# Slot attention's first and last round: the order of five engines' work around them

## What is computed

```python
x = x + 0.5 * L0_ffn(ln(x))     # mixture of 8 experts, top 2          phase moe_a
x = x + L0_attn(ln(x))          # causal linear attention, 16 heads    phase linatt
x = x + 0.5 * L0_ffn(ln(x))     #                                      phase moe_b
x = x + 0.5 * L1_ffn(ln(x))     # gated FFN, both operands fp4-rounded phase ffn_a
x = x + L1_attn(ln(x))          # softmax attention over the 8 batches phase att
x = x + 0.5 * L1_ffn(ln(x))     #                                      phase ffn_b

# L1_attn takes S = 8 (the batches) as its sequence: each token position ("slot")
# has 16 heads whose 8 x 8 scores run over the batches
scores = einsum('sbd,tbd->bst', q, k) * scale;  attn = softmax(scores)
ctx = einsum('bst,tbd->sbd', attn, v);  out = ctx @ out_proj.T + bias
# L1_ffn: h = silu(q4(x) @ q4(w_gate).T) * (q4(x) @ q4(w_up).T);  out = q4(h) @ q4(w_down).T
# q4 rounds blocks of 16 values to an fp4 grid times the block's scale
```

## Time and profile before

| what | us |
|---|---|
| median of 3 runs (lowest, highest) | 759.08 (758.55, 763.17) |
| the profiled execution | 757.82 |
| its span in the profile | 756.0 |
| busy in the span: PE, DVE, ACT, POOL | 673.3, 606.9, 458.5, 294.7 |
| mean granted TensorE clock | 0.959 of 2.4 GHz |

### The profile page before, as it was taken

How to read it: one execution, slowest core, us unless ns; L and a number is a source line. 1 busy time by engine, 2 the same in 40 slices (tenths; PEclk the granted TensorE clock), 3 DMA queues, 4 the chain that set the end, 5 groups by cost and what they waited for, 6 DMA issues and landing times.

```text
span 756.0 us, 16397 instructions
## 1 busy us (share of the span) xinstructions
PE 673.3 (89%) x5826; PEld 481.9 (64%) x5826; DVE 606.9 (80%) x1554; ACT 458.5 (61%) x867; POOL 294.7 (39%) x417
## 2 busy tenths in 40 slices
PE   4999999789999879999997789898978987799996
PEld 2777776567888757777764456565646556456664
DVE  2788787846766678887786999999999997899983
ACT  3787788674674328777786476757454433666642
POOL 5000120156556310011013677554534527668520
PEclk9999999879999989999999799999999998899996
DMA  8000000000000000000000000000000000000000
GB/s 207 22 0 0 0 1 1 0 3 4 2 0 3 4 1 1 0 0 0 0 1 2 0 1 0 1 2 0 3 0 0 0 0 1 0 29 15 24 19 29
DMA packets 13461, 7.08 MB, mean 9 GB/s; under 512 B 1177, under 2 KB 13409, under 8 KB 13409
## 3 DMA queue, kind: packets, MB, share of 16 engines
q1 hardware_dynamic: 11328, 5.33, 2.6%
q10 hardware_dynamic: 2080, 1.05, 0.5%
HBM read 4.28 MB, written 2.10 MB: 8 GB/s over the span
## 4 chain that ended last, share of the span: by engine, by line
PE 61%; DVE 18%; ACT 10%; issue 7%; POOL 3%; DMA 1%; DVEq 0%; POOLq 0%; ACTq 0%
PE ps L1427 56%; DVE shared L1267 4%; DVE shared L1239 3%; PE ps L1778 2%; DVE x_sb L1070 2%; ACT ffn_work L533 2%; ACT ffn_work L723 2%; PE ps L1435 1%; DVE stats L985 1%; ACT xnT L584 1%; ACT x_sb L832 1%; PE ps L1441 1%; ACT ffn_work L571 1%; ACT hqT L828 1%; DVE ps L1259 1%
## 5 line engine op out<-in xcount | busy, mean ns | idle before, releaser
L1427 PEld LDWEIGHTS ps<-w_sb,sq_h 128*128 128x128 f32 x1024 | 132.3, 193 | 70.6 <-ACT sq_h L599 51.8
L1070 DVE SCALAR_TENSOR_TENSOR x_sb<-ps,gates,x_sb 128x128 f32 (+1 forms) x512 | 147.2, 344 | 24.2 <-PE ps L1427 20.3
L1427 PE MATMUL ps<-w_sb,sq_h 128*128 128x128 f32 x1024 | 138.5, 279 | 1.8 <-ACT sq_h L599 1.8
L1427 PE MATMUL ps<-xnT,w_sb 128*128 128x512 f32 x256 | 135.7, 614 | 0.0
L353 POOL TENSOR_SCALAR vareps<-meanvar 128x4 f32<-128x4 f32 (+1 forms) x28 | 8.9, 319 | 265.7 <-DVE meanvar L994 265.3
L595 ACT ACTIVATE relu_h<-ps 128x512 f32<-128x512 f32 x128 | 75.6, 591 | 56.5 <-PE ps L1427 56.2
L599 ACT ACTIVATE sq_h<-relu_h 128x512 f32<-128x512 f32 x128 | 80.6, 630 | 4.0
L1427 PE MATMUL ps<-gateT,xnT 128*128 128x352 f32 x128 | 58.9, 544 | 14.7 <-ACT ffn_work L723 13.0
L577 ACT ACTIVATE xn<-x_sb,shift,rstd 128x128 f32 (+1 forms) x136 | 57.0, 481 | 10.1 <-POOL shift L361 8.3
L400 POOL TENSOR_TENSOR shared<-shared 128x128 f32<-128x128 f32 x112 | 51.0, 455 | 27.7 <-ACT shared L678 19.5
L1427 PE MATMUL ps<-downT,hqT 128*128 128x128 f32 x384 | 57.5, 289 | 4.2 <-ACT hqT L828 3.9
(11 more groups left out here) (166 smaller groups left out, 1355.9 us busy)
## 6 DMA issues: line engine op xcount, KB each, us to landing
x_sb<-in_L_attn_x_dram SPq DMA_DIRECT2D x8, 256.0 KB, 7.5
out_dram<-x_sb SPq DMA_DIRECT2D x8, 256.0 KB, 2.3
w_sb<-in_L_ffn_w_all_dram ACTq DMA_DIRECT2D x2, 512.0 KB, 6.5
wraw<-in_L_attn_qkv_w_dram SPq DMA_DIRECT2D x1, 192.0 KB, 4.4
wraw<-attn_in_proj_weight_dram SPq DMA_DIRECT2D x1, 192.0 KB, 3.3
fraw<-in_L_ffn_w_down_dram SPq DMA_DIRECT2D x1, 176.0 KB, 3.1
fraw<-in_L_ffn_w_gate_dram SPq DMA_DIRECT2D x1, 128.0 KB, 2.7
fraw<-in_L_ffn_w_up_dram SPq DMA_DIRECT2D x1, 128.0 KB, 2.4
```

The costliest lines, as they stand in the source:

```text
L1070: t = nc.vector.scalar_tensor_tensor(tile_b(i, j), bank(4 + e % 4, TPB, C)[:, j, :], gates[:, j, e:e + 1], tile_b(i, j), ALU.mult, ALU.add)
L1427: return nc.tensor.matmul(o, a, b, start=start, stop=stop, **kw)
```

## The change

It moves instructions; it adds and takes away none but waits. PE and ACT: score(0, 0) and its copy stand in the last body of ffn_a, score and copy of half 0 of every other round at the end of the round before. In the last round x_transposes and gate_up of tile 0 (with bank 3 for the gate) stand behind context 1, the other three gate_up ahead of contexts 4 to 7. ACT's evac_xnT goes ahead of normal(1), silu of tile 0 ahead of ctx_half(0), and ctx_half(1) behind the other silu, x_squares(1) and x_offsets(1). POOL's x_back(0) goes from behind pair 3 to behind pair 1, DVE's x_snap(0) from behind pv 3 to behind pv 1. In moe_b, the statistics in group 6 go from behind accumulate(5) to behind accumulate(4).

```diff
@@ POOL, the last round of att
                     slot_pairs(s, TPB - 1, 0, 2)
+                    ffn_b.x_back(0)
                     ffn_b.layer_norm(1)
-                    slot_pairs(s, TPB - 1, 2, 4)
-                    ffn_b.x_back(0)
-                    slot_pairs(s, TPB - 1, 4, B)
+                    slot_pairs(s, TPB - 1, 2, B)
@@ ACT, att: body and last_body
                 def body(i, more, ahead2):
-                    scores_half(i, 0)
                     exp_half(i, 0)
-                    scores_half(i, 1)
+                    front.scores_half(i, 1)
...
                     x_out(i, 0)
                     x_out(i, 1)
+                    front.scores_half(i + 1, 0)
 
                 def last_body(i):
-                    scores_half(i, 0)
                     exp_half(i, 0)
-                    scores_half(i, 1)
+                    front.scores_half(i, 1)
                     x_squares(nxt, 0)
                     x_offsets(nxt, 0)
                     exp_half(i, 1)
+                    evac_xnT(nxt, 0, k=2)
                     normal(nxt, False, 1)
+                    silu(nxt, 0, 0, 3)
                     ctx_half(i, 0)
                     x_out(i, 0)
-                    evac_xnT(nxt, 0, k=2)
-                    for j in range(TPB):
+                    for j in range(1, TPB):
                         silu(nxt, 0, j, 6)
-                    ctx_half(i, 1)
                     x_squares(nxt, 1)
                     x_offsets(nxt, 1)
+                    ctx_half(i, 1)
                     x_out(i, 1)
@@ ACT, ffn: body
                         normalise(front.s, g - GROUPS + 2, B, tile_t, B // 2)
+                    if first and g == GROUPS - 1:
+                        front.scores_half(0, 0)
@@ DVE, moe
-                        if e == 5 and more:
+                        if more and e == (5 if ahead or first else 4):
@@ DVE, att: body
                     pv(i, 0)
                     pv(i, 1)
+                    if not more:
+                        x_snap(nxt, 0)
                     less_max(i, 1)
...
                     pv(i, 3)
-                    if not more:
-                        x_snap(nxt, 0)
                     normal(i, 1)
@@ PE, att: body
                 def body(i, more):
-                    score(i, 0)
-                    turn(i, 0)
-                    score(i, 1)
+                    front.score(i, 1)
                     if more:
                         front.transposes_b(i + 1)
-                    turn(i, 1)
+                    front.turn(i, 1)
...
                     for b in range(4):
                         context(i, b)
+                        if not more and b == 1:
+
+                            pe.wait_ge(front.s["lin_ready"], 6 * TPB)
+                            x_transposes(nxt, 0, 2)
+                            gate_up(nxt, 0, 0, 3)
                     if more:
                         front.make_v(i + 1)
                     project_out(i, 0)
                     if not more:
-
-                        pe.wait_ge(front.s["lin_ready"], 6 * TPB)
-                        x_transposes(nxt, 0, 2)
+                        for j in range(1, TPB):
+                            if j > 1:
+
+                                pe.wait_ge(s["pv_ready"], B * i + 4 * (j - 1))
+                            gate_up(nxt, 0, j, 6)
                     for b in range(4, B):
                         context(i, b)
-                        if not more:
-                            if b >= 6:
-
-                                pe.wait_ge(s["pv_ready"], B * i + 4 * (b - 5))
-                            gate_up(nxt, 0, b - 4, 6)
                     project_out(i, 1)
+                    if more:
+                        front.score(i + 1, 0)
+                        front.turn(i + 1, 0)
 
+                front.turn(0, 0)
                 pe.wait_ge(S["ffn_a"]["x_done"], GROUPS)
@@ PE, ffn: body
                     hidden_transposes(g, 3)
+                    if first and g == GROUPS - 1:
+
+                        pe.wait_ge(s["hT_ready"], g * TPB + 3)
+                        front.score(0, 0)
                     down(g, 2)
```

More of the change, by code:

```diff
@@ L750, in take_v, with scores_half @@
                     self.take(i, 5, v_att, None)
+                def scores_half(self, i, k):
+                    act.wait_ge(self.s["score_done"], 2 * i + k + 1)
+                    nc.scalar.activation(turned[:, 4 * k:4 * k + 4, :], bank(6 + k, 4, P),
+                                         ACT.Copy).then_inc(self.s["scT_ready"], 1)
             def att(s, front, nxt):
@@ L757, in exp_half @@
                                          scale=float(HD) ** -0.5).then_inc(s["exp_ready"], 1)
-                def scores_half(i, k):
-                    act.wait_ge(s["score_done"], 2 * i + k + 1)
-                    nc.scalar.activation(turned[:, 4 * k:4 * k + 4, :], bank(6 + k, 4, P),
-                                         ACT.Copy).then_inc(s["scT_ready"], 1)
                 def ctx_half(i, k):
@@ L1691, in make_v, with score @@
                         t.then_inc(self.s["lin_done"], 1)
-            def att(s, front, nxt):
-                def score(i, k):
-                    pe.wait_ge(s["qk_ready"], B * i + 4 * k + 4)
+                def score(self, i, k):
+                    pe.wait_ge(self.s["qk_ready"], B * i + 4 * k + 4)
                     for odd in range(2):
@@ L1703, in score, with turn, att @@
                                    start=odd == 0, stop=odd == 1, tile_position=(0, CH * pair))
-                    t.then_inc(s["score_done"], 1)
-                def turn(i, k):
-                    pe.wait_ge(s["scT_ready"], 2 * i + k + 1)
+                    t.then_inc(self.s["score_done"], 1)
+                def turn(self, i, k):
+                    pe.wait_ge(self.s["scT_ready"], 2 * i + k + 1)
                     for j in range(4):
                         t = nc.tensor.transpose(bank(4 + k, 4, P)[:, j, :], turned[:, 4 * k + j, :], ident[:, :])
-                    t.then_inc(s["sc_turned"], 1)
+                    t.then_inc(self.s["sc_turned"], 1)
+            def att(s, front, nxt):
                 def context(i, b):
```

## The result

The changed kernel takes 752.02 us (median of 4, 749.25 to 753.83) against 759.06 for the kernel before on the same occasions: 7.0 less, where 7.1 was forecast, at 752.0. The ratio is 0.9892, 95% interval 0.9845 to 0.9940. Measured again later with six runs it was 751.25 and 0.9896 (0.9866 to 0.9925). The ratio is not the quotient of the two medians, which is 0.9907 here and 0.9888 in the later measurement. So the change is about one per cent, a little beyond it by the ratios, and the intervals reach to both sides: the times don't decide between the 0.42 that the prediction gave to more than one per cent and its 0.57 for less.

A forecast was written before the change was run, and what follows sets the result against it. No engine is full and the bound changes by stage; the gain is how much sooner DVE passes three joints, 1.0 + 1.9 + 4.2 = 7.1 us, giving 752.0 us, range 749.5 to 755.5.

The forecast's parts named there:

- moe_b, 1.0: In moe_b, statistics one expert sooner bring DVE's gates and the accumulation 1.0 us sooner; bounds 0 and 1.3.
- First round, 1.9: First round of att: score(0, 0) among the last down products cuts DVE's 2.09 us wait before less_max by 1.9.
- Rival (e): First round: x_out(7) goes back as much as score comes forward, so 1.9 becomes 0; total 5.2, 753.9 us; chance 0.06.
- hid(0) of ffn_b at 637.6, bound by DVE: Last round: hid of group 0 starts at 637.6 instead of 643.35, 5.75 us sooner, waiting for DVE rather than PE.
- gate_up of group 1 4.2 sooner: In ffn_b, PE's gate_up of group 1 starts at 645.6 instead of 649.79, behind contexts, x_out, normal(2) and evac_xnT.
- hid(1) 4.2 sooner: In ffn_b, hid of group 1 starts at 653.85 instead of 658.03 if PE's four gate_up take as long as before.
- One sign that the prediction had named for being wrong: Last round: x_out(3, 1) ends less than 1 us sooner relative to DVE's pv 7 than before.
- the other sign: In ffn_b: hid(0) still waits for PE over 1 us at the full clock.
- (a): Rival: clock stays up before group 1 of ffn_b, DVE binds; tail 5.8, total 8.7, 750.4 us; chance 0.25.
- (b): Rival: clock falls mid last round and delays all behind it; tail 1.9, total 4.8, 754.3 us; chance 0.18.
- (c): Rival: the tail gives nothing back, work only exchanged; 2.9 us left, 756.2 us; chance 0.07.
- (d): Rival: low clock holds from context 2 until project_out(1), kernel 1.7 us slower, 760.8 us; chance 0.04.

The follow-up runs named there:

- the second execution: The changed kernel, unaltered, measured again later with six runs and profiled: 751.25 us, ratio 0.9896 to the kernel before.
- the kernel with early gates and late rounding: Against the changed kernel, only POOL's x_back(0) and DVE's x_snap(0) put back behind pair 3 and pv 3: 758.68 us, ratio 1.0011 to the kernel before.
- the silu experiment: Changed kernel with normal(2) ahead of ctx_half(1), plus ACT's four silu of group 0 ahead of x_squares(1) in ffn_a: 743.84 us, ratio 0.9807 to the kernel before.

## Why the prediction was right

It was right in total and in the path of each term; of the sizes, that of moe_b was a third too large and those of the tail came out partly by errors that cancelled. That the median lies within 0.1 of 752.0 is luck: the four runs scatter from 749.25 to 753.83, and the profiled execution, forecast at 750.7, took 752.95, as 2.3 were added ahead of all three joints.

- *moe_b, 1.0*: 0.68 in the first profile, 0.6 in the mean at equal clock. The mechanism held: ACT waited 0.43 (0.55 forecast), the down product came 0.93 sooner and the next one 1.09 (at most 0.93 and about 1.1 forecast), and the exponential 1.04. What was overlooked is that DVE's gates would then fall on POOL's x_divide(0): this gives 0.36 back.
- *First round, 1.9*: 1.87, and 1.7 by undoing it. x_out(7) went back by as much as was worked out, and it is what releases DVE now. Rival (e) is excluded.
- *hid(0) of ffn_b at 637.6, bound by DVE*: counted from the last round's less_max that is 23.2; it came at 23.58, bound by PE (a wait of 1.45). So the step "now bound by DVE itself" failed, though it cost only 0.4. x_snap(0) took 0.85, not 1.6, and with 0.2 from another instruction DVE was free a us sooner. The clock fell near 627 for some 3 us: gate_up(0) took 2.5 instead of 1.4. And each later gate_up took 1.47, not 1.41. Even in the second execution, where the clock stayed up, hid(0) at 22.92 is bound by PE, with a wait of 0.78.
- *gate_up of group 1 4.2 sooner*: 646.08 against 649.79, with the 0.22 by which this profile's last round starts sooner taken off 3.5. The 0.7 missing is the same fall of the clock: in the second execution, where it stayed up, gate_up of group 1 starts 31.22 behind the last round's less_max, against 35.37 before and 31.88 here, which is 4.15. The chain was the one named, and DVE's new wait for normal(2) was 1.51 (1.0 forecast). Before, another chain had ended last there: x_snap(1) stands behind hid(0) on DVE, POOL's x_back(1) behind it, and PE's x_transposes of group 1 waited for that, as the timeline of PE before shows:

```profile
648.42 0.63 PE L1441 MATMUL ps<-ident,xn 128*128 128x128 f32 x4 [3.41 <-POOL xn L453]
```

- *hid(1) 4.2 sooner*: 4.58. Here the forecast took the old 8.2 us at mostly half clock for the four gates; they took 7.1, since only the middle of them (647.65 to 650.5) ran at 1.2 GHz. This gave back what the row above lost.

One sign that the prediction had named for being wrong did appear: x_out(3, 1) ends 10.84 us behind the end of pv 7 instead of 11.59, only 0.75 sooner (1.42 in the second execution; the prediction's own times give 2.3). Half of what is missing is x_snap(0), whose shorter time brought pv 7 forward by 0.8; counted from the last round's less_max, x_out(3, 1) ends 1.5 sooner, and 2.2 in the second execution. The rest is mostly the fall of the clock. The sign was badly chosen, since x_out(3, 1) did not bound gate_up of group 1 before, and the other sign, hid(0) waiting over 1 us for PE at the full clock, did not appear (1.45 with the clock down, 0.78 with it up).

Of the rivals, (a) and (b) are not other outcomes but the ends between which executions of this one kernel lie: the tail was 39.03 and 38.54, where (a) asked for 37.8 and (b) for 41.7. (c) and (d) didn't happen. The slower side that the prediction missed is the one that the kernel with early gates and late rounding shows: 2 us lost, the low clock included, which the sum contained only as the time 625.3 at which x was ready. It also missed the longest wait, 6.65 before hid(0) of ffn_a, which the silu experiment shows to be worth over 4 us.

The Trainium skill's rule on the shared port pair (SBUF — State Buffer, Who interferes with whom) fits the rows: x_snap got the pair ahead of POOL's second addition and took 0.85, and POOL's two additions took 2.94 instead of the 2.50 of the kernel with late rounding. The rule had given 0.7 for this case and 1.9 for the other; which of them occurs is a matter of which instruction starts first, and I had taken a value near the wrong one. The 0.55 of the gates fits it too.

## What to carry to other kernels

An instruction with a late input holds up all behind it on its engine: look in each list for a wait ahead of work whose input is ready, above all where ACT or POOL feed PE (silu behind x_squares cost over 4 us here, normal(2) behind x_out about 2). Moving a consumer forward paid here only with its producer moved too; either alone gave nothing or lost. And in a kernel with a changing clock read the gain from the distance between two instructions of the bounding engine, where a tenth shows, rather than from times that scatter by several us.

## What was not expected

The same instructions, up to the rank of group 6 of moe_b, took between 373.9 and 379.9 us in the profiled executions of these kernels, though nothing was changed ahead of it. Of the 5.0 us between the two profiles of the changed kernel 3.0 arise there, so a good part of the 6 us over which its runs scatter (747.88 to 753.98) can come from there. In the two profiles compared above, 0.8 of the 2.3 arises within the first 31 us and 1.0 between 235 and 295; from 230 to 290 the granted clock was 0.91 after and 0.94 before. The places at which the clock falls after a hole in PE's work aren't fixed to the program. The Trainium skill says (TensorE: Matmul & The Clock Gate, Part 1), of the slow matmuls after a kernel's start, that the same kernel can have a different number of them from run to run. In these runs the same holds in the middle of the kernel: the first gate of the last round took 1.54 in one execution of the changed kernel and 0.86 in another.
